# Expert slots of a two-layer gated model: 39 slots or 36, eleven of them shared by two experts

## The reference, cut to what matters

```
xf = layernorm(x).reshape(2048, 256)
scores = softmax(xf @ w_router)                      # 8 experts
expert_weights, expert_indices = top_k(scores, 2)    # two experts a token
h = silu(xf @ w1[e]) * (xf @ w3[e]);  y = h @ w2[e]  # 256 -> 512 -> 256
moe = sum over the two experts of weight * y
shared = silu(xf @ ws1) * (xf @ ws3) @ ws2
x = x + tanh(g_ffn[1]) * (shared / 3 + moe * 2 / 3)
```

## Time and profile before

| | us |
|---|---|
| three runs | 752.92, 748.81, 751.78 (median 751.78) |
| profiled execution, in all | 748.97 |
| its span, first to last instruction | 747.0 |
| TensorE busy | 713.1 (95%) |
| VectorE, ScalarE, GpSimd busy | 404.8, 274.7, 119.5 |
| mean granted TensorE clock | 0.98 of 2.4 GHz |

### The profile page before, as it was taken

One profiled execution on the slowest core, in us unless ns is written; L12 is line 12 of the kernel. 1 busy time (PEld: TensorE's weight loads), 2 busy tenths in 40 slices (PEclk: granted clock), 3 DMA queues, 4 the chain that ended last, 5 costly groups with the idle time before them and its releaser, 6 DMA issues.

```text
span 747.0 us, 11555 instructions
## 1 busy us (share of the span) xinstructions
PE 713.1 (95%) x3562; PEld 509.9 (68%) x3563; DVE 404.8 (54%) x1028; ACT 274.7 (37%) x605; POOL 119.5 (16%) x133
## 2 busy tenths in 40 slices
PE   8999999999899997899999999999999999999991
PEld 8767777777644344799998566568888866666661
DVE  4688877888336558988887363212323323333330
ACT  3544444344454444667775321111122112222220
POOL 2100000000000001000000006640223332322232
PEclk9999999999999999899999999999999999999997
DMA  9670000000070000084002003336555422223221
GB/s 298 171 264 15 1 0 0 0 0 0 1 226 0 0 1 1 1 297 155 0 0 64 22 1 107 110 124 213 159 116 148 106 37 50 42 44 48 47 31 21
DMA packets 47398, 54.59 MB, mean 73 GB/s; under 512 B 8532, under 2 KB 36006, under 8 KB 47364
## 3 DMA queue, kind: packets, MB, share of 16 engines
q1 hardware_dynamic: 40020, 44.41, 18.7%
q0 software_dynamic: 7344, 9.75, 7.8%
HBM read 37.35 MB, written 16.79 MB: 72 GB/s over the span
## 4 chain that ended last, share of the span: by engine, by line
PE 89%; DVE 5%; ACT 2%; DMA 1%; issue 1%; POOL 0%; SPq 0%; POOLq 0%; ACTq 0%; DVEq 0%
PE ps L481 80%; PE ps L484 10%; DVE work L1638 1%; DVE stats L1516 1%; DVE maxes L1637 1%; DMA early<-in_wk 1%; DVE x_rows L1761 1%; DMA out_rows<-work,out_index 1%; ACT work L1138 0%; ACT late L1138 0%; ACT work L1220 0%; POOL out_rows L465 0%; DVE work L1659 0%; DVE den L1657 0%; DVE early L1752 0%
## 5 line engine op out<-in xcount | busy, mean ns | idle before, releaser
L481 PE MATMUL ps<-middle,work 128*128 128x256 f32 (+3 forms) x824 | 215.3, 411 | 2.4 <-ACT work L1138 1.2
L481 PEld LDWEIGHTS ps<-middle,work 128*128 128x128 f32 x824 | 151.4, 190 | 48.3 <-issue 28.4
L1138 ACT ACTIVATE work<-ps 128x512 f32<-128x512 f32 (+3 forms) x214 | 85.0, 434 | 213.4 <-PE ps L484 200.8
L484 PE MATMUL ps<-consts_sb,work 128*128 128x128 f32 x600 | 89.6, 284 | 6.4 <-ACT late L1138 2.6
L484 PEld LDWEIGHTS ps<-consts_sb,work 128*128 128x128 f32 x600 | 72.0, 144 | 32.9 <-issue 17.7
L481 PE MATMUL ps<-late,work 32*128 32x154 f32 (+3 forms) x704 | 82.2, 311 | 1.7 <-ACT work L1138 0.6
L481 PE MATMUL ps<-work,late 128*128 128x256 f32 (+1 forms) x416 | 82.6, 353 | 1.2 <-ACT work L1138 1.2
L481 PE MATMUL ps<-early,late 128*128 128x512 f32 (+2 forms) x192 | 77.6, 608 | 0.3 <-ACT early L1289 0.3
L481 PEld LDWEIGHTS ps<-work,late 128*128 128x128 f32 x416 | 71.0, 193 | 9.9 <-ACT work L1138 1.6
L481 PE MATMUL ps<-early,work 128*128 x168 | 76.1, 596 | 0.8 <-ACT work L1138 0.8
L481 PEld LDWEIGHTS ps<-late,work 128*128 128x128 f32 (+1 forms) x704 | 70.9, 191 | 7.4 <-issue 1.4
(11 more groups left out here) (189 smaller groups left out, 634.6 us busy)
## 6 DMA issues: line engine op xcount, KB each, us to landing
late<-in_w SPq DMA_DIRECT2D x18, 512.0 KB
early<-in_w SPq DMA_DIRECT2D x16, 512.0 KB, 10.5
expert_rows<-work SPq DMA_DIRECT2D x39, 130.0 KB, 2.7
work<-expert_rows SPq DMA_DIRECT2D x39, 130.0 KB, 2.2
middle<-in_w SPq DMA_DIRECT2D x8, 512.0 KB, 8.1
out_rows<-x_rows SPq DMA_DIRECT2D x4, 512.0 KB
x_rows<-in_x SPq DMA_DIRECT2D x2, 768.0 KB, 11.4
late<-in_ws SPq DMA_DIRECT2D x3, 512.0 KB, 3.8
```

The source lines that it names most:

```text
L481: return nc.tensor.matmul(o, l, r, start=start, stop=stop, **kw)
L484: return nc.tensor.transpose(o, i, ident[0:rows, 0:rows])
L1138: return nc.scalar.activation(o, i, ACT.Copy)
```

## The change

Rows are assigned in halves of 64. Each expert's rows are cut into twos of tiles, then at most one whole tile, then one or two halves; halves of different experts can share a tile. Then 36 tiles are always enough. `DOUBLES` stays 9, `LEFT` becomes 18: the first 7 (`WHOLE`) are still of one expert, the other 11 may have one expert in rows 0 to 63 and another in rows 64 to 127, and are always computed as two halves. `parts` does that: two matmuls with 64 stationary columns each, into PSUM rows 0 to 63 and 64 to 127, the first with the weights of the lower half's expert from SBUF, the second with those of the upper half's, which SyncE loads for w1 and w3 into `wb` (`load_second`, 1 MB a tile) and ScalarE copies for w2 into `w2b` (`second_w2`).

- The order becomes: 7 whole singles, 11 mixed singles, 9 pairs. The row loads of the first tiles and pair come ahead of the last two stores, the second weights of tiles 7 and 8 behind them, and the other rows behind those.
- `slots` grows from 17 small operations to 28 ahead of the row indices, `slot_experts` gets another comparison.
- Results have four buffers `yo` and `to` in place of two. A mixed tile is added in two indirect DMAs of 64 rows, one after the other has landed; the two tiles of a pair are added without a wait between them. `turn` is gone, GpSimd's and VectorE's loops over the singles are written out, and the last wait for the additions is SyncE's, no longer GpSimd's.

```diff
-SLOTS = 2 * B * S // P + NE - 1
+HALF_T = P // 2
+SLOTS = ((2 * B * S + NE * (HALF_T - 1)) // HALF_T + 1) // 2
+WHOLE = (2 * B * S - NE * (P - 1) + P - 1) // P - ONE
...
+            def load_second(i, k):
+                s = 2 * i + k
+                if isinstance(s, int) and s < WHOLE + 2:
+                    sp.wait_ge(q["s_h"], 2 * FC * NG)
+                else:
+                    sp.wait_ge(q["e_h"], 2 * s - 2)
+                e = sp.value_load(sei[HALF_T:HALF_T + 1, bass.ds(s + ONE, 1)], min_val=0, max_val=NE - 1)
+                for w, src in enumerate((w1, w3)):
+                    sp.dma_start(wb[k % 2][:, w, :, :], src[bass.ds(e, 1), :, :].rearrange("a (k p) n -> p (a k) n", p=P)
+                                 ).then_inc(q[f"h_ld{k % 2}"], 16)
...
+            load(0, 0)
+            load(0, 1)
             load_two(0, 0)
...
             store(NG - 2)
             store(NG - 1)
+            sp.wait_ge(q["r_exp"], 1)
+            load_second(3, 1)
+            load_second(4, 0)
+            with sp.Fori(1, 4) as i:
+                load(i, 0)
+                load(i, 1)
+            load(4, 0)
+            with sp.Fori(4, 8) as i:
+                load_second(i, 1)
+                load(i, 1)
+                load_second(i, 2)
+                load(i, 2)
...
+            for n in range(LEFT):
+                pool.wait_ge(q["e_yc"], n + 1)
+                after(pool, q["e_add"], adds(n))
+                if n < WHOLE:
+                    accumulate(to[n % 4][:, 0:1], yo[n % 4])
+                else:
+                    accumulate(to[n % 4][0:HALF_T, 0:1], yo[n % 4][0:HALF_T, :])
+                    pool.wait_ge(q["e_add"], adds(n) + 16)
+                    accumulate(to2[n % 4][:, 0:1], yo[n % 4][HALF_T:P, :])
+            for j in range(DOUBLES):
+                pool.wait_ge(q["e_add"], adds(LEFT + 2 * j))
+                for u in range(2):
+                    pool.wait_ge(q["e_yc"], LEFT + 2 * j + u + 1)
+                    pool.wait_ge(q["e_to"], LEFT + 2 * j + u + 1)
+                    accumulate(to[2 * (j % 2) + u][:, 0:1], yo[2 * (j % 2) + u])
...
+            def parts(o, left, m, first_w, second_w, k, n):
+
+                for h, w in enumerate((first_w, second_w)):
+                    last = mm(o[HALF_T * h:HALF_T * h + HALF_T, :], left[:, m, HALF_T * h:HALF_T * h + HALF_T], w,
+                              k == 0, k == n - 1)
+                return last
...
             pe.wait_ge(q["s_hs"], 4 * NG - 1)
-            d_trans(0, 0)
+            e_trans(0, 0)
             s_down(NG - 1, 0)
+            e_trans(0, 1)
             s_down(NG - 1, 1)
...
+            e_up(0, 0)
+            e_up(0, 1)
+            e_trans(0, 2)
+            e_hidden_t(0, 0)
+            for n in range(2, 7):
+                e_step(n // 2, n % 2)
+            e_step(3, 1, up=True)
+            e_step(4, 0, up=True)
+            with pe.Fori(4, 8) as i:
+                e_step(i, 1, up=True, down=True)
+                e_step(i, 2, up=True, down=True)
+            e = e_up(8, 1, 15, True)
+            e_hidden_t(8, 0)
+            d_trans(0, 0)
+            e_down(8, -1, e, True)
+            e = d_up(0, 0, LEFT - 2 + ONE)
+            e_hidden_t(8, 1)
             d_trans(0, 1)
+            e_down(8, 0, e, True)
+            e_down(8, 1, None, True)
             d_step(0, 1)
...
+            def second_w2(i, k):
...
+                e = act.value_load(sei[HALF_T:HALF_T + 1, bass.ds(s + ONE, 1)], min_val=0, max_val=NE - 1)
+                copy(w2b[k % 2].rearrange("p f d -> p (f d)"),
+                     w2s[:, bass.ds(e, 1), :, :].rearrange("p a f d -> p (a f d)")).then_inc(q["h_w2"], 1)
...
             def d_yo(i, k):
                 j = 2 * i + k
+                if isinstance(j, int):
+                    dve.wait_ge(q["e_add"], adds(LEFT + 2 * max(0, j - 1)))
```

More of the change, by code:

```diff
@@ L248, in build @@
         wb = [cut(late, 3072 * p, [2, KD, F]) for p in range(2)]
+        w2b = [cut(late, 3072 * p + 2048, [FC, D]) for p in range(2)]
         sil2 = [cut(work, 3600 + 256 * f, [2 * P]) for f in range(FC)]
-        hT2 = [cut(work, 4624 * p, [FC, 2 * P]) for p in range(2)]
+        hT2 = [cut(late, 6144, [FC, 2 * P]), cut(work, 4624, [FC, 2 * P])]
         sil = [cut(work, 3600 + 512 * p, [F]) for p in range(2)]
@@ L253, in build @@
         hT = [cut(work, 512 * p, [FC, P]) for p in range(2)]
-        yo = [cut(work, 1024 + 256 * p, [D]) for p in range(2)]
+        yo = [cut(masks, 1600 + 256 * p, [D]) for p in range(4)]
         seed = cut(masks, 3700, [B, NK])
@@ L417, in _ @@
             load_weights(DOUBLES // 2, 0)
[L418 to L423, removed]
+            sp.wait_ge(q["e_add"], adds(SLOTS))
         @block.gpsimd
@@ new lines, in e_up @@
+            def e_up(i, k, lagging=None, mixed=False):
+                s = 2 * i + k
+                p = k % 2
+                pe.wait_ge(q["e_xt"], s + 1)
+                after(pe, q["e_hh"], s - 1)
+                if mixed:
+                    pe.wait_ge(q[f"h_ld{p}"], 32 * (i + (k - 7) // 2 + 1))
+                e = expert_of(s + ONE)
+                for w in range(2):
+                    o = ps[:, 2 * p + w, :]
+                    for m in range(KD):
+                        own = w13[:, bass.ds(e, 1), w, m, :].rearrange("p a n -> p (a n)")
+                        if mixed:
+                            last = parts(o, xgT[p], m, own, wb[p][:, w, m, :], m, KD)
+                        else:
+                            last = mm(o, xgT[p][:, m, :], own, m == 0, m == KD - 1)
+                    last.then_inc(q["e_h"], 1)
+                    if w == 0 and lagging is not None:
+                        lagging = expert_of(lagging + ONE)
+                return lagging
@@ L1036, in d_down, with d_step @@
                     last.then_inc(q["d_y"], 1)
-            def d_step(i, k, nxt=True):
+            def d_step(i, k):
                 e = d_up(i, k, 2 * (2 * i + k - 1))
-                if nxt:
-                    d_trans(i, k + 1)
+                d_trans(i, k + 1)
                 d_down(i, k - 1, e)
[L1044 to L1075, removed]
-                    pe.wait_ge(q["e_yc"], ONE)
-                after(pe, q["e_hTa"], s)
-                after(pe, q["e_hTv"], s)
-                for u in range(2):
-                    for f in range(2):
-                        last = tr(ps[:, 5 + u, P * f:P * f + P], hh[k % 2][:, P * (2 * u + f):P * (2 * u + f) + P])
-                    last.then_inc(q["e_th"], 1)
@@ L1909, in slots @@
[L1909 to L1910 removed]
+                seq(v.tensor_scalar(lim[:], cnt[:, 0, :], 2.0 * P, None, ALU.mult))
+                seq.mark(v.tensor_tensor(esc[:], order, spread(lim[:], 1, full), ALU.is_ge))
+                seq(v.tensor_scalar(cnt[:, 1, :], rem[:], float(P), None, ALU.is_ge))
+                seq.mark(v.scalar_tensor_tensor(rem2[:], cnt[:, 1, :], -1.0 * P, rem[:], ALU.mult, ALU.add))
```

413 lines of the change are left out of this document (219 added, 194 removed).

## The result

The changed kernel takes 759.75 us (median of 10 runs, 753.39 to 763.16), the kernel before 750.11 us (10 runs, 745.33 to 752.92): ratio 1.0126, 95% interval 1.0096 to 1.0156. It is slower by 1.3%. The profiled execution has a span of 758.2 us, 760.05 in all: 11.2 more span than before and 21.1 more than the 737.1 of the sum.

The account below looks back on a forecast made before the run. TensorE's instructions were taken to bound the kernel, busy 713.1 of 747.0 us. The terms summed to -9.9: 737.1 of span, 739.1 in all, plus 2 for the median: 741 us, range 733 to 752.

Parts of the forecast that it names:

- Output additions: GpSimd's additions of the mixed tiles: 3.3 us per half, 73 us in all against 78 available, so hidden.
- rival C: GpSimd's additions bind once a half addition takes over 3.55 us: 751 at 4.0, 758 at 4.3; chance 0.12.
- Eleven tiles in two halves: TensorE in the mixed singles: the two half products run side by side, so the halves add nothing.
- Rival D: Half products on TensorE not quite side by side, weight loads showing: 764 us, fully serial 798; chance 0.08.
- Changing the array's shape: TensorE switching between whole transposes and half products: 13 pairs of changes at 0.31 us, +4.0 us (3 to 7).
- Routing: More small operations in `slots` ahead of the expert stage make the first rows later: +0.8 us (0 to 1.9).
- The third tile's rows: TensorE waits before the third tile's transposes for rows queued behind stores and weights: +5.2 us (0 to 7).
- The clock: A stretch at half clock brought by the 5 us hole before the third tile: +1.7 us (0 to 3.4).
- Waits in the chain: TensorE: 0.69 us before the second pair's products goes, 0.5 before the last mixed tile's second product comes: -0.2 us.
- Second weights: In mixed tiles, rows queued behind second w1 and w3 have 0.6 us of room: +1.0 us taken (0 to 5).
- Rival E: Each mixed tile waits for its rows behind its weights, 0.5 to 1 us a tile: 746 to 752, chance 0.10.
- Tail: After the last matmul, additions overlap and SyncE waits for their landing: end at 10.0 us instead of 14.9, -4.9.

Follow-up runs that it names:

- no loads: The changed kernel without the weight loads of tiles 9 to 17, which reuse the second weights of tiles 7 and 8: 748.5 us, ratio 1.0002.
- copies: The changed kernel with the mixed tiles' second w1 and w3 copied inside SBUF by ScalarE and VectorE instead of loaded from HBM: 742.72 us, ratio 0.9929.

## Why the prediction was wrong

The direction was wrong: faster was given 0.77 (by the rivals' own shares it is 0.79), and the 759.75 lies above the range of 733 to 752. The step that failed is *Output additions*, and in it one size: "For 64 rows I take h = 3.3: issue and data shrink, latency doesn't (bounds 1.9 ... and 4.3 ...)", and so "Hidden, with 5 to spare." The wait, its place and the threshold held; it was rival C, given 0.12 and priced up to 758.

- The room was right: 78 us were forecast from the first half addition to TensorE's stop. Measured 99.75 less the stop of 19.16: 80.6.
- h was 4.53, above even the upper bound. In three parts. First, a half addition with no traffic lands at 3.1, not far under a whole one's 3.8: halving the rows saves 0.13 of the issue (1.42 against 1.55) and some 0.55 of the rest. My 3.3 was about right for that, but it left out GpSimd's restart behind a landing, 0.27 and in every second one 0.71 us (the chain's "issue"), which makes 3.4 and 3.9, mean 3.66. Second, 0.9 us more on the mean from weight traffic. I had seen it, "now DMA is two thirds busy beside it", and gave it no price: the upper bound was a whole addition in quiet, and bounds from quiet rows bound nothing once the change itself adds the traffic. Third, TensorE's steps have no part in it that the runs show: with whole products in their place h was 4.34 and the time the same.
- By the prediction's own rule, 2.2 us for each 0.1 above 3.55, 4.53 costs 21.6; measured were 19.2 of stop and 1.5 of slow products behind it. With 3.96 (no loads) the rule says 9, with 3.92 (copies) 8; the stop was 7.8 in both.

The other terms, with what they measured:

- *Three tiles fewer*: a whole single still steps by 5.82 us (545.26 to 551.08), so the 17.5 came.
- *Eleven tiles in two halves*: nothing was taken; the halves' records start 0.01 us apart (554.47 and 554.48 above), and eight such pairs in a row step by 0.43 us each, so their weight loads stayed hidden. Rival D is refuted. The Trainium skill (TensorE: Matmul & The Clock Gate, Part 3: Packing small matmuls — row/col tiling) says in its list of what overlaps that a weight load does so only when the row groups differ. For column halves with rows in common the trace disagrees. The Trainium skill also says in that section, under The mechanism, that a load into the background weight buffer is pulled ahead of running matmuls. With that the trace agrees.
- *Changing the array's shape*: mixed steps of 6.12 (557.14 to 563.26), forecast 6.13; that is 3.3 us over the eleven, and the 0.6 taken for the hand-over to the pairs was not measured by itself.
- *Routing*: the first transposes at 501.89, 0.56 after the earlier trace rows; forecast 0.8. But over the variants this start lies between 500.8 and 506.0, so a single execution can't confirm a term of this size.
- *The third tile's rows*: 4.98, forecast 5.2, and the landing at 521.3, forecast 521.7. The two versions with nine buffers, with and without it, differ by about this and its half clock.
- *The clock*: half clock from 518.6 to 525.4, about 1.9 lost, forecast 1.7; and again behind the stop, which no term had.
- *Waits in the chain*: 0.78 before the last mixed tile's second product, where 0.5 was put; the 0.69 is gone, so the sum of the two is +0.1 and not -0.2.
- *Second weights*: 1.0 was taken; in the changed kernel no mixed tile waited for its second weights and one for its rows, 0.64 us (601.51 above). Rival E did not happen.
- *Tail*: from the end of the last matmul at 746.7 to 758.2 are 11.5; forecast 10.0. The last addition was issued at 749.57, 0.6 later than counted, and from the end of that issue the closing took 7.1, not 6.5.

With the measured sizes in place of mine the sum is -17.5 + 3.3 + 0.6 + 5.0 + 1.9 + 0.1 + 0.6 - 3.4 + 19.2 + 1.5 = +11.3, and the profiled span grew by 11.2. Without the last two terms it would be -9.4, close to the -9.9 of the prediction; that it is so close is partly luck, since the errors of the tail and of the smaller terms cancel.

## What to carry to other kernels

When work is reordered so that a serial chain on another engine grows (here 11 additions to 22), price the chain under the traffic that the change itself adds, not by a row from a quiet stretch, and give the upper bound that price; where the margin is 5 us of 78, the duration has to be known to 7%. Look at what the two periodic streams do in phase: the same load that passed between the additions when both were released by one step ran into 10 of 22 of them when they followed one another. More buffers postpone a debt rather than remove it, and only if every wait is moved with them: here the second pair's wait stood where it was, though its buffers were free. If data already lies on the chip, a copy by engines with idle time (here ScalarE, 37% busy, and VectorE, 53%) keeps the queues free for those who wait on latency.

## What the runs showed of the hardware that I had not expected

- An indirect addition to HBM lands in 3.1 us for 64 rows and 3.8 for 128 with less than 0.05 MB beside it, and in 5.1 and 6.0 beside 0.7 MB or more on SyncE's queue (means; only 5 such whole ones).
- Half the rows save only 0.13 us of GpSimd's issue (1.42 against 1.55 us).
- A stop of 19 us brought the clock down from 658.5 to 675.6, 17 us, 2.9 of them behind the stop.
- The quiet stretch at the end runs from GpSimd's last issue: moving its last wait to SyncE took 2.1 us off the end (12.85 for 14.9).
